# Convolution attention in query halves: two key tiles of the weighted sum together, three score banks, four single maxima banks

## The chip, the cores and the metric

The kernel runs on one core of one Trainium2 chip. The metric is the device time of one execution in microseconds. All the work of the change lies in one of the program's phases, the attention inside the convolution layer.

## What is computed

The whole program is a convolution layer with attention, then a second attention layer and a feed-forward layer. The change touches the first attention alone. For each of 8 images and 8 heads (head dimension 8, 1024 tokens), cut from the reference:

```python
logits = jnp.einsum('bnid,bnjd->bnij', qf, kf)      # 1024 x 1024 per head
logits = logits + rel_w + rel_h                     # relative positions, width and height
weights = jax.nn.softmax(logits, axis=-1)
attn = jnp.einsum('bnij,bnjd->bnid', weights, vf)
```

The softmax needs the maximum of each query's row before the exponentials can be taken.

## The kernel before, in words

`attention_phase` works in 16 groups (image by half of the heads), each of `HG` = 4 heads, `TT` = 8 tiles of 128 tokens and two query halves of `HALF` = 512 tokens. The relative positions are folded into the matmul: `qf` and `kf` hold 120 rows, and a 121st row of `qf` (`ROW_M`) carries minus the maximum of each query.

Each group is handled twice.

- **The first pass** finds the maxima, one group ahead of the rest. `logits` multiplies a query tile with all 1024 keys into one of two `sm` tensors, each two PSUM banks wide (two matmuls, L664). VectorE reduces its 1024 columns to `nmax` (`logits_max`, L644). That makes 32 steps a group. After the 16 steps of a pair of heads, the unit called "turn" transposes the pair's `nmax` on TensorE (L679), VectorE copies it to `mrow` (L657), and SyncE sends eight small DMAs that put it into row `ROW_M` of `qf` (`maxima`, L639).
- **The second pass** computes the scores transposed, keys on the partitions: `scores` (L880) writes one of two `st` banks, one per query half; ScalarE takes the exponential into `probs` (L855); `weighted` (L895) multiplies four heads' `probs` with the values `va` into `pv`. The four heads use 32 columns of the array each and run beside each other. These matmuls are fp32, and the trace shows each as two, so one call is 8 records: two waves of four.

Every engine runs its own queue in program order, and semaphores tie them. TensorE's order is written by hand in `period`, for each pair of (key tile, head) steps:

```python
for half in range(2):
    scores(n, j, s, half)
weighted(n, j, t - 1, h // 2)
for half in range(2):
    scores(n, j, s + 1, half)
for step in (s, s + 1):
    for half in range(2):
        first_pass(pe, n + 1, (j + 1) % BUFS, ahead, step, half)
```

So a group has 16 such rounds, each of four score matmuls, one weighted call and four first-pass matmuls. `scores` waits for the exponential of two matmuls before (`exp_done`), `logits` for the reduction two steps before (`sm_read`), and a turn for the last reduction of its pair. A turn comes twice a group, at first-pass steps 12 and 28 (16 and 32 less `AHEAD` = 4). The last group has no first pass beside it. The groups run in a loop of three (`all_groups`), four times around, with the first and the rest written out.

The first pass of group 0 runs earlier, in a block of its own, together with the matmuls of the relative positions; its order is the list `order`.

Of the kernel before, what the change touches and what calls it, by code (L numbers as in the profile page):

```python
# [11 lines left out]
P = 128  # L12
# [529 lines left out]
def attention_phase(nc, q_all, bd_hi, bd_lo, shared, first_stored, kq_d, rel_d, va_d, att_d):  # L542
# [12 lines left out]
    with ExitStack() as ctx:  # L555
# [7 lines left out]
        kf = [sb(f"a_kf{i}", [P, HG, TOK], f32r) for i in range(BUFS - 1)]  # L563
        nmax = sb("a_nmax", [P, HG, TT])
        mrow = sb("a_mrow", [2 * TT, HG // 2, P], f32r)

        sm = [ctx.enter_context(nc.psum_tensor(f"a_sm{i}", [P, TOK], f32)) for i in range(2)]
# [5 lines left out]
        sm_done, sm_read = sem("a_sm_done"), sem("a_sm_read")  # L573
# [9 lines left out]
        def first_pass_units(whole):  # L583
            units, step = [], 0
            for d, h, t in [(0, h, t) for h in range(HG) for t in range(TT)][AHEAD:] + [(1, 0, t) for t in range(AHEAD) if whole]:
                if t == 0 and h % 2 == 0:
                    units.append((step, "turn", 0, (h - 1) % HG, 0))
                units.append((step, "logits", d, h, t))
                step += 1
            return units if whole else units + [(step, "turn", 0, HG - 1, 0)]  # L590
        first_pass_of = {whole: first_pass_units(whole) for whole in (True, False)}
        NU = len(first_pass_of[True])
        unit_at = {whole: {unit[1:]: k for k, unit in enumerate(units)} for whole, units in first_pass_of.items()}
        units_before = lambda n: AHEAD + n * NU
        STEPS = TT * HG
        NS = 2 * STEPS

# [35 lines left out]
        def maxima(sp, n, j, whole):  # L633

            for h in range(HG):
                for half in range(2):
                    if half == 0:
                        sp.wait_ge(sm_read, units_before(n) + unit_at[whole]["turn", 0, h | 1, 0] + 1)
# [3 lines left out]
        def logits_max(dve, before, k, h, t):  # L642
            dve.wait_ge(sm_done, before + k + 1)
            nc.vector.tensor_reduce(nmax[:, h, t:t + 1], sm[k % 2][:], axis=AX.X, op=ALU.max, negate=True).then_inc(sm_read, 1)  # L644

        def first_pass_maxima(dve, n, whole, only=None):
            for k, (step, what, d, h, t) in enumerate(first_pass_of[whole]):
                if only not in (None, step):
                    continue
                if what == "logits":  # L650
                    logits_max(dve, units_before(n), k, h, t)
                else:
                    dve.wait_ge(sm_done, units_before(n) + k + 1)
# [3 lines left out]
                    nc.vector.tensor_copy(mrow[:, h // 2, :], sm[k % 2][0:2 * TT, 0:P]).then_inc(sm_read, 1)  # L657

        def logits(pe, j, before, k, h, t, half):

            if half == 0 and not (isinstance(before, int) and before + k < 2):
                pe.wait_ge(sm_read, before + k - 1)
            cols = slice(half * HALF, (half + 1) * HALF)
            m = nc.tensor.matmul(sm[k % 2][:, cols], qf[j][0:ROW_M, h, half, t * P:(t + 1) * P],  # L664
                                 kf[j][0:ROW_M, h, cols], start=True, stop=True)
            if half == 1:
                m.then_inc(sm_done, 1)

        def first_pass(pe, n, j, whole, s, half, va_after=0):

            for k, (step, what, d, h, t) in enumerate(first_pass_of[whole]):
                if step == s and what == "logits":
# [3 lines left out]
                elif step == s and half == 0:  # L676
                    pe.wait_ge(sm_read, units_before(n) + k - 1)
                    pe.wait_ge(sm_read, units_before(n) + unit_at[whole]["logits", 0, h, TT - 1] + 1)
                    nc.tensor.transpose(sm[k % 2][0:2 * TT, 0:P], nmax[:, h - 1:h + 1, :].rearrange("p h t -> p (h t)"), ident[:]).then_inc(sm_done, 1)  # L679
# [12 lines left out]
        passes = [("logits", 0, t) for t in range(AHEAD)] + [("pass", s, None) for s in range(STEPS)]  # L692
# [11 lines left out]
        with (nc.sbuf_tensor("a_hl", [P, 2, LAST, TOK], f32r) as own_hl, nc.psum_tensor("a_rel0", [P, 4, LAST, W], f32) as r0,  # L704
# [51 lines left out]
            def _(dve):  # L756
# [4 lines left out]
                for what, i, n in order:  # L761
# [5 lines left out]
                    elif what == "logits":  # L767
                        logits_max(dve, 0, n, 0, n)
                    else:
                        first_pass_maxima(dve, 0, True, i)  # L770

            @block.tensor
            def _(pe):
                for what, i, n in order:
# [15 lines left out]
                    for half in range(2):  # L790
                        if what == "logits":
                            logits(pe, 0, 0, n, 0, n, half)
                        else:
                            first_pass(pe, 0, 0, True, i, half, va_after=16)
# [4 lines left out]
        probs = bits(shared[:])  # L799
        out = sb("a_out", [P, TOK])  # L800
        st = [ctx.enter_context(nc.psum_tensor(f"a_st{i}", [P, HALF], f32)) for i in range(2)]
        pv = ctx.enter_context(nc.psum_tensor("a_pv", [P, TOK], f32))

        with nc.Block() as block:  # L804
# [36 lines left out]
            def _(act):  # L841
                def copy_out(n, half):
                    cols = slice(half * HALF, (half + 1) * HALF)
                    act.wait_ge(pv_done, n * 2 * TT + 2 * TT + 3 + half)
                    if half == 0:
                        act.wait_ge(out_stored, n * 16 + 16)
                    nc.scalar.activation(out[:, cols], pv[:, cols], ACT.Copy).then_inc(out_ready, 1)

                def period(n, j, more, ahead):
                    for u in range(NS):  # L850
                        t, h, half = u // (2 * HG), u // 2 % HG, u % 2
                        act.wait_ge(st_done, n * NS + u + 1)
                        if h == half == 0:
                            act.wait_ge(pv_done, n * 2 * TT + 2 * t + 2)
                        nc.scalar.activation(probs[:, t % 2, h, half * HALF:(half + 1) * HALF], st[half][:], ACT.Exp  # L855
                                             ).then_inc(exp_done, 1)
                        if u in (3, 7) and not (isinstance(n, int) and n == 0):
                            copy_out(n - 1, u // 4)

                all_groups(act, period)  # L860
                for half in range(2):
                    copy_out(NG - 1, half)
# [10 lines left out]
            def _(pe):  # L873
                def scores(n, j, s, half):

                    t, h = s // HG, s % HG
                    pe.wait_ge(exp_done, n * NS + 2 * s + half + 1)
                    if t == half == 0:
                        pe.wait_ge(max_loaded[h], n * 32 + 32)
                    nc.tensor.matmul(st[half][:], kf[j][0:ROW_M + 1, h, t * P:(t + 1) * P],  # L880
# [3 lines left out]
                def weighted(n, j, t, half):  # L884


                    if half == 0:
                        pe.wait_ge(exp_done, n * NS + 2 * HG * (t + 1) + 2)
                    if t == half == 0:
                        pe.wait_ge(loaded[j], times_loaded(n, j))  # L890
                    if t == 0:
                        pe.wait_ge(out_ready, n * 2 + half + 1)
                    cols = slice(half * HALF, (half + 1) * HALF)
                    for h in range(HG):
                        m = nc.tensor.matmul(pv[32 * h:32 * h + 32, cols], va[j][:, t, h, :], probs[:, t % 2, h, cols],  # L895
# [3 lines left out]
                def period(n, j, more, ahead):  # L899
                    for s in range(0, STEPS, 2):  # L900
                        t, h = s // HG, s % HG
                        for half in range(2):
                            scores(n, j, s, half)
                        if t:
                            weighted(n, j, t - 1, h // 2)
                        elif not (isinstance(n, int) and n == 0):
                            weighted(n - 1, (j - 1) % BUFS, TT - 1, h // 2)
                        for half in range(2):
                            scores(n, j, s + 1, half)
                        if more:  # L910
                            for step in (s, s + 1):
                                for half in range(2):
                                    first_pass(pe, n + 1, (j + 1) % BUFS, ahead, step, half)

                pe.sem_inc(exp_done, 2)
# [3 lines left out]
                for half in range(2):  # L919
                    weighted(NG - 1, (NG - 1) % BUFS, TT - 1, half)  # L920
# [952 lines left out]
```

## Time and profile before

| | us |
|---|---|
| runs | 2534.36, 2540.37, 2546.37 (median 2540.37) |
| span of the profiled execution | 2543.5 |
| part in which the groups run | 647 to 1475 |
| block before it, with the first pass of group 0 | 545 to 647 |

The profile gives no other time of its execution than its span, which lies 3.1 us above the median and inside the three runs. In the profile, DVE is VectorE, ACT ScalarE, PE a matmul and PEld its weight load; an entry like "[0.25 <-DVE a_nmax L644]" is the time that the engine stood idle just before, and what ended it. One row may merge several instructions (x4).

### The profile page before, as it was taken

Reading aid. Unit: us, or ns where it says so; the run is one execution under the profiler, and the core shown is the slowest. Engines: PE = TensorE matmul, PEld = TensorE weight load, DVE = VectorE, ACT = ScalarE, POOL = GpSimd, SP = SyncE. Lnnn points to the kernel's source line nnn. Section 1 sums busy time; section 2 is a strip of 40 time slices with the busy share of each in tenths; the row PEclk is TensorE's granted clock in tenths of the full one; section 3 lists DMA queues with packets and bytes.
Section 4 is the critical chain, followed back from the end, with each engine's and each line's share of the span. In section 5 each row is a group of like instructions: output and inputs, shape, how many; then the busy total and the mean of one; then the engine's idle time right before and its main releaser. Section 6 shows DMA issues by size and latency. Waiting matters only on the chain. (4 is left out here: it accounts for less than half of the span.)

```text
span 2543.5 us, 33099 instructions
## 1 busy us (share of the span) xinstructions
PE 2209.1 (87%) x10534; PEld 1523.3 (60%) x10534; DVE 1506.6 (59%) x2238; ACT 1188.2 (47%) x2087; POOL 332.1 (13%) x161
## 2 busy tenths in 40 slices
PE   4999999846899999999999838888888948888885
PEld 3778888745445454544554316777777736676664
DVE  6222433326677777777777214665556448888885
ACT  2111222212567676766777725555555434444342
POOL 1000000000000000000000012222222024444443
PEclk7999999855899999999999969999999979999988
DMA  2222243495757665676564033232221142222221
GB/s 78 87 62 80 85 157 132 133 162 198 153 91 123 106 105 92 112 117 99 101 107 73 9 86 111 96 97 94 95 95 50 50 130 83 84 83 83 83 89 52
DMA packets 155219, 249.54 MB, mean 98 GB/s; under 512 B 30912, under 2 KB 101312, under 8 KB 155072
## 3 DMA queue, kind: packets, MB, share of 16 engines
q1 hardware_dynamic: 153760, 247.05, 40.2%
q8 instruction: 75, 1.23, 0.2%
q10 hardware_dynamic: 1312, 0.67, 0.1%
q14 instruction: 72, 0.59, 0.1%
HBM read 154.52 MB, written 90.47 MB: 96 GB/s over the span
## 5 line engine op out<-in xcount | busy, mean ns | idle before, releaser
L644 DVE TENSOR_REDUCE a_nmax<-a_sm 128x1 f32<-128x1024 f32 x512 | 603.7, 1219 | 221.7 <-PE a_sm L664 221.5
L855 ACT ACTIVATE shared<-a_st 128x512 f32<-128x512 f32 x1024 | 556.6, 596 | 256.1 <-PE a_st L880 254.5
L895 PE MATMUL a_pv<-shared,a_va 128*32 128x512 f32 x2048 | 274.0, 608 | 0.9 <-ACT shared L855 0.9
L880 PE MATMUL a_st<-a_qf,a_kf 121*128 121x512 f32 x704 | 255.3, 440 | 18.8 <-issue 8.5
L664 PE MATMUL a_sm<-a_kf,a_qf 120*128 120x512 f32 x704 | 218.5, 429 | 57.5 <-DMA a_kf<-kq_d 32.9
L880 PEld LDWEIGHTS a_st<-a_qf,a_kf 121*128 121x128 f32 x704 | 120.1, 190 | 219.0 <-ACT shared L855 197.7
L664 PEld LDWEIGHTS a_sm<-a_kf,a_qf 120*128 120x128 f32 x704 | 136.0, 203 | 95.4 <-issue 33.0
L1707 ACT ACTIVATE x_hid<-x_h_ps,x_b 128x512 f32<-128x512 f32 x128 | 87.5, 689 | 213.5 <-DVE x_h_lo L1744 129.0
L1744 DVE SCALAR_TENSOR_TENSOR x_h_lo<-x_hid,x_wts,x_h_hi 128x512 fp32r<-128x512 f32 x128 | 175.3, 1370 | 9.6
L1742 DVE TENSOR_SCALAR x_h_hi<-x_hid,x_wts 128x512 fp32r<-128x512 f32 x128 | 114.9, 898 | 45.3 <-ACT x_hid L1707 40.4
L1153 POOL MEMSET b_wp<- 128x128 f32 x1 | 0.2, 204 | 977.5 <-POOLq L804 977.5
L1785 PE MATMUL x_h_ps<-x_v_hi,x_w_hi 128*128 128x512 f32 x256 | 106.7, 417 | 17.7 <-POOL x_w_lo L1673 17.4
L1355 PE MATMUL b_o_ps<-b_pT,b_v 128*128 128x256 f32 x512 | 120.7, 379 | 0.0
L1276 DVE TENSOR_REDUCE b_nmax<-b_s_ps 128x1 f32<-128x1024 f32 x64 | 78.4, 1224 | 69.4 <-PE b_s_ps L1340 62.8
L1799 PE MATMUL x_y_ps<-x_h_hi,x_w_hi 128*128 128x512 f32 x256 | 103.2, 403 | 17.9 <-DVE x_h_lo L1744 17.9
L507 PE MATMUL c_acc<-c_y_hi,c_w_hi 128*128 128x512 f32 x288 | 117.6, 408 | 0.0
L507 PE MATMUL c_acc<-c_y_hi,c_w_hl 128*128 128x512 f32 x288 | 117.2, 407 | 0.0
L507 PE MATMUL c_acc<-c_y_lo,c_w_hi 128*128 128x512 f32 x288 | 117.1, 407 | 0.0
L507 PE MATMUL c_acc<-c_y_lo,c_w_hl 128*128 128x512 f32 x288 | 117.1, 407 | 0.0
L507 PE MATMUL c_acc<-c_y_hi,c_w_lo 128*128 128x512 f32 x288 | 117.1, 406 | 0.0
L1186 ACT ACTIVATE b_probs<-b_s_ps,b_nmax 128x1024 f32<-128x1024 f32 x64 | 71.3, 1113 | 95.8 <-DVE b_nmax L1276 95.8
L880 PE MATMUL a_st<-q_all,a_kf 121*128 121x512 f32 x320 | 112.5, 433 | 0.3 <-ACT shared L855 0.3
(253 smaller groups left out, 4045.6 us busy)
## 6 DMA issues: line engine op xcount, KB each, us to landing
rel_d<-shared SPq DMA_DIRECT2D x12, 2048.0 KB, 12.2
a_qf<-rel_d SPq DMA_DIRECT2D x44, 512.0 KB
x_w_st<-in_L_ffn_W SPq DMA_DIRECT2D x32, 512.0 KB, 5.9
a_qf<-rel_d SPq DMA_DIRECT2D x44, 256.0 KB
q_all<-rel_d SPq DMA_DIRECT2D x20, 512.0 KB
a_qf<-kq_d SPq DMA_DIRECT2D x66, 128.0 KB
c_xtok<-in_x SPq DMA_DIRECT2D x8, 1024.0 KB, 5.6
va_d<-c_va SPq DMA_DIRECT2D x16, 512.0 KB, 4.8
```

What stands on the lines that cost most here:

```text
L507: m = nc.tensor.matmul(image_rows(acc[u][:]), wt[:, k, :] if tap is None else wt[:, k, tap, :], y[s][:, k, rows + dy:rows + dy + H // 2, d ...
L644: nc.vector.tensor_reduce(nmax[:, h, t:t + 1], sm[k % 2][:], axis=AX.X, op=ALU.max, negate=True).then_inc(sm_read, 1)
L664: m = nc.tensor.matmul(sm[k % 2][:, cols], qf[j][0:ROW_M, h, half, t * P:(t + 1) * P], kf[j][0:ROW_M, h, cols], start=True, stop=True)
L855: nc.scalar.activation(probs[:, t % 2, h, half * HALF:(half + 1) * HALF], st[half][:], ACT.Exp).then_inc(exp_done, 1)
L880: nc.tensor.matmul(st[half][:], kf[j][0:ROW_M + 1, h, t * P:(t + 1) * P], qf[j][0:ROW_M + 1, h, 2 * t // TT, half * HALF:(half + 1) * HALF ...
L895: m = nc.tensor.matmul(pv[32 * h:32 * h + 32, cols], va[j][:, t, h, :], probs[:, t % 2, h, cols], start=t == 0, stop=t == TT - 1, skip_gro ...
L1355: m = nc.tensor.matmul(o_ps[:], v_sb[s][:, t, :], pT[k % 2][:, t, :], start=t == 0, stop=t == TT - 1)
L1707: nc.scalar.activation(hid[k % 2][:], h_ps[k % 2][:], ACT.Gelu, bias=b1_sb[s][:, e, f:f + 1]).then_inc(hid_ready, 1)
L1742: nc.vector.tensor_scalar(h_hi[k % HB][:], hid[k % 2][:], wts[s][:, e:e + 1], None, ALU.mult)
L1744: nc.vector.scalar_tensor_tensor(h_lo[k % HB][:], hid[k % 2][:], wts[s][:, e:e + 1], bits(h_hi[k % HB][:]), ALU.mult, ALU.subtract).then_i ...
L1785: m = nc.tensor.matmul(h_ps[k % 2][:], w[s][:, e, c, tile(f)], v[s][:, c, half(j)], start=i == 0, stop=i == 3 * KC - 1)
L1799: m = nc.tensor.matmul(y_ps[j][c][:], w[s][:, e, f, tile(c)], h[k % HB][:], start=first and i == 0, stop=last and i == 2)
```

## The change

Nothing changes in what is computed. Parts:

- **First pass in halves.** `sm` is four tensors of one bank (`SB` = 4) in place of two of two banks. A step is now half the keys: one matmul, one reduction of 512 columns into `nmax_half`. There are 64 steps a group. After a pair's last reduction VectorE drains and takes the minimum of both halves (`tensor_tensor`, 128x16) into `nmax`, and signals `nmax_ready`, for which the turn waits. Turns stand at steps 24 and 56 and take two bank slots.
- **Second pass by query halves.** All 8 key tiles for the first 512 queries, then all 8 for the second. A unit is one matmul of one head; three `st` banks (`STB` = 3) are used in turn; `pv` is one bank; `probs` has four slots.
- **TensorE's order** is a string for each batch of 8 score units (8 batches a group): s is a score matmul, m a first-pass step, v a weighted call.
- ScalarE copies `pv` out after the 8th and the 40th exponential of a group, before after the 4th and the 8th.

```diff
+        SB = 4
+        sm = [ctx.enter_context(nc.psum_tensor(f"a_sm{i}", [P, HALF], f32)) for i in range(SB)]
...
+        STB = 3
+        SLOTS = 4
+        BATCH = 2 * HG
+        NB = NS // BATCH
+        ORDER = "mssmsmsvvsmsmmsmsm"
...
-            nc.vector.tensor_reduce(nmax[:, h, t:t + 1], sm[k % 2][:], axis=AX.X, op=ALU.max, negate=True).then_inc(sm_read, 1)
+            nc.vector.tensor_reduce(nmax_half[:, half, h, t:t + 1], sm[k % SB][:], axis=AX.X, op=ALU.max, negate=True).then_inc(sm_read, 1)
+            if h % 2 and t == TT - 1 and half:
+                dve.drain()
+                nc.vector.tensor_tensor(nmax[:, h - 1:h + 1], nmax_half[:, 0, h - 1:h + 1], nmax_half[:, 1, h - 1:h + 1], ALU.min
+                                        ).then_inc(nmax_ready, 1)
...
-            if half == 0 and not (isinstance(before, int) and before + k < 2):
-                pe.wait_ge(sm_read, before + k - 1)
+            if not (isinstance(before, int) and before + k < SB):
+                pe.wait_ge(sm_read, before + k + 1 - SB)
...
+                    pe.wait_ge(sm_read, units_before(n) + k + 1 - SB)
+                    pe.wait_ge(nmax_ready, n * (HG // 2) + (h + 1) // 2)
+                    nc.tensor.transpose(sm[k % SB][0:2 * TT, 0:P], nmax[:, h - 1:h + 1, :].rearrange("p h t -> p (h t)"), ident[:]).then_inc(sm_done, 2)
...
-        st = [ctx.enter_context(nc.psum_tensor(f"a_st{i}", [P, HALF], f32)) for i in range(2)]
-        pv = ctx.enter_context(nc.psum_tensor("a_pv", [P, TOK], f32))
+        st = [ctx.enter_context(nc.psum_tensor(f"a_st{i}", [P, HALF], f32)) for i in range(STB)]
+        pv = ctx.enter_context(nc.psum_tensor("a_pv", [P, HALF], f32))
...
+                def scores(n, j, u):
+
+                    half, t, h = u // (TT * HG), u // HG % TT, u % HG
+                    pe.wait_ge(exp_done, n * NS + u + 1)
...
+                    for i in range(NB):
+                        place = dict.fromkeys("smv", 0)
+                        for what in ORDER:
+                            k = place[what]
+                            place[what] += 1
+                            if what == "s":
+                                scores(n, j, i * BATCH + k)
+                            elif what == "m" and more:
+                                first_pass(pe, n + 1, (j + 1) % BUFS, ahead, i * BATCH + k)
+                            elif what == "v" and i:
+                                weighted(n, j, 2 * (i - 1) + k)
+                            elif what == "v" and not (isinstance(n, int) and n == 0):
+                                weighted(n - 1, (j - 1) % BUFS, 2 * (NB - 1) + k)
```

On TensorE, one round of before in the middle of a group reads as follows (a_st are the score banks, a_sm the first-pass ones, a_pv the weighted sum; a REGISTER_ALU works out what a wait compares with):

```order
L895 MATMUL a_pv<-shared,a_va0 32x512 x4
L877 REGISTER_ALU
L880 MATMUL a_st0<-a_qf0,a_kf0 128x512
L877 REGISTER_ALU
L880 MATMUL a_st1<-a_qf0,a_kf0 128x512
L662 REGISTER_ALU
L664 MATMUL a_sm1<-a_kf1,a_qf1 128x512 x2
L662 REGISTER_ALU
L664 MATMUL a_sm0<-a_kf1,a_qf1 128x512 x2
L877 REGISTER_ALU
L880 MATMUL a_st0<-a_qf0,a_kf0 128x512
L877 REGISTER_ALU
```

The same engine after the change, the middle of a batch:

```order
L896 MATMUL a_st1<-q_all,a_kf2 128x512
L678 REGISTER_ALU
L680 MATMUL a_sm0<-a_kf0,a_qf0 128x512
L893 REGISTER_ALU
L896 MATMUL a_st2<-q_all,a_kf2 128x512
L909 MATMUL a_pv<-shared,a_va2 32x512 x8
L893 REGISTER_ALU
L896 MATMUL a_st0<-q_all,a_kf2 128x512
L678 REGISTER_ALU
L680 MATMUL a_sm1<-a_kf0,a_qf0 128x512
```

Two weighted calls now stand together, once in 8 score matmuls rather than one in 4, and score and first-pass matmuls alternate.

At a turn, TensorE before (the rows ahead of the transpose are the weighted call and the two scores that follow it; the last first-pass matmul stands two scores ahead of that call):

```order
L880 MATMUL a_st0<-a_qf0,a_kf0 128x512
L877 REGISTER_ALU
L880 MATMUL a_st1<-a_qf0,a_kf0 128x512
L895 MATMUL a_pv<-shared,a_va0 32x512 x4
L877 REGISTER_ALU
L880 MATMUL a_st0<-a_qf0,a_kf0 128x512
L877 REGISTER_ALU
L880 MATMUL a_st1<-a_qf0,a_kf0 128x512
L677 REGISTER_ALU
L678 REGISTER_ALU
L679 MATMUL a_sm1<-a_ident,a_nmax 16x128
```

and after the change:

```order
L896 MATMUL a_st0<-q_all,a_kf2 128x512
L678 REGISTER_ALU
L680 MATMUL a_sm1<-a_kf0,a_qf0 128x512
L694 REGISTER_ALU
L695 REGISTER_ALU
L696 MATMUL a_sm2<-a_ident,a_nmax 16x128
L678 REGISTER_ALU
L680 MATMUL a_sm0<-a_kf1,a_qf1 128x512
```

The pair's last first-pass matmul (L680) now stands directly ahead of the transpose that waits for its reduction; four scores and a weighted call stood between them before.

## Rows read from the trace of the kernel before

**Rows 1.** The page: engines' busy time; two groups (busy, mean ns | idle before).

```profile
PE 2209.1 (87%) x10534; PEld 1523.3 (60%) x10534; DVE 1506.6 (59%) x2238; ACT 1188.2 (47%) x2087; POOL 332.1 (13%) x161
...
L644 DVE TENSOR_REDUCE a_nmax<-a_sm 128x1 f32<-128x1024 f32 x512 | 603.7, 1219 | 221.7 <-PE a_sm L664 221.5
L855 ACT ACTIVATE shared<-a_st 128x512 f32<-128x512 f32 x1024 | 556.6, 596 | 256.1 <-PE a_st L880 254.5
```

**Rows 2.** Windows: busy time in two steady groups and the last.

```profile
core 0: us, PE busy (x) PEld busy (x) DVE busy (x) ACT busy (x) POOL busy (x), PEclk, DMA share, GB/s
776.90:827.13 50.23, 50.15 (x258) 25.11 (x258) 38.24 (x35) 35.54 (x67) 0.00 (x0) 1.00 0.66 108
...
1425.20:1474.80 49.60, 41.61 (x196) 12.82 (x196) 0.00 (x0) 35.08 (x66) 0.00 (x0) 1.00 0.03 11
```

**Rows 3.** SyncE's timeline: start of the maxima DMAs of two following groups.

```profile
776.90 27.74 SPq L639 DMA_DIRECT2D a_qf<-a_mrow  x8
...
827.13 27.65 SPq L639 DMA_DIRECT2D a_qf<-a_mrow  x8
```

**Rows 4.** Timeline of one round (start us, us, engine ..., [idle before]).

```profile
936.47 1.06 PE L895 MATMUL a_pv<-shared,a_va 128*32 128x512 f32 x8
937.46 0.30 PEld L880 LDWEIGHTS a_st<-q_all,a_kf 121*128 121x128 f32 x2 [0.84 <-ACT shared L855]
938.00 1.09 ACT L855 ACTIVATE shared<-a_st 128x512 f32<-128x512 f32 x2 [0.53 <-PE a_st L880]
...
938.70 2.35 DVE L644 TENSOR_REDUCE a_nmax<-a_sm 128x1 f32<-128x1024 f32 x2 [0.75 <-PE a_sm L664]
...
939.14 0.19 PEld L880 LDWEIGHTS a_st<-q_all,a_kf 121*128 121x128 f32 x1 [0.22 <-ACT shared L855]
939.41 1.08 ACT L855 ACTIVATE shared<-a_st 128x512 f32<-128x512 f32 x2 [0.32 <-PE a_st L880]
...
939.58 1.07 PE L895 MATMUL a_pv<-shared,a_va 128*32 128x512 f32 x8
```

**Rows 5.** Timeline of the next round in short windows.

```profile
940.03 0.61 PE L895 MATMUL a_pv<-shared,a_va 128*32 128x512 f32 x4
940.57 0.19 PEld L880 LDWEIGHTS a_st<-q_all,a_kf 121*128 121x128 f32 x1 [0.84 <-ACT shared L855]
...
941.14 0.40 PE L664 MATMUL a_sm<-a_kf,a_qf 120*128 120x512 f32 x1
...
941.14 1.10 PE L664 MATMUL a_sm<-a_kf,a_qf 120*128 120x512 f32 x4
```

**Rows 6.** Timeline at a turn, and a small VectorE operation (ns min/median/max).

```profile
826.32 0.09 PEld L679 LDWEIGHTS a_sm<-a_ident,a_nmax 128*16 128x16 f32 x1 [0.24 <-DVE a_nmax L644]
826.82 0.28 DVE L657 CAST a_mrow<-a_sm 16x128 fp32r<-16x128 f32 x1 [0.56 <-PE a_sm L679]
827.15 0.30 PEld L664 LDWEIGHTS a_sm<-a_kf,a_qf 120*128 120x128 f32 x2 [0.50 <-DVE a_mrow L657]
...
L50 DVE TENSOR_TENSOR b_tmp<-b_tmp,b_var x16: 161/164/166, 1515.9 to 1964.9; 128x4 f32<-128x4 f32 x16
```

**Rows 7.** Timeline of a round in the last group.

```profile
1430.32 0.30 PEld L880 LDWEIGHTS a_st<-a_qf,a_kf 121*128 121x128 f32 x2 [0.84 <-ACT shared L855]
...
1431.51 0.19 PEld L880 LDWEIGHTS a_st<-a_qf,a_kf 121*128 121x128 f32 x1 [0.89 <-ACT shared L855]
...
1433.41 0.30 PEld L880 LDWEIGHTS a_st<-a_qf,a_kf 121*128 121x128 f32 x2 [0.84 <-ACT shared L855]
```

**Rows 8.** Timeline and windows after three gaps on TensorE (columns of Rows 2).

```profile
858.82 0.31 PEld L880 LDWEIGHTS a_st<-a_qf,a_kf 121*128 121x128 f32 x2 [3.05 <-issue]
...
860.50:863.40 2.90, 2.90 (x10) 2.17 (x7) 0.59 (x1) 1.60 (x4) 0.00 (x0) 0.50 0.00 0
...
2131.16 0.50 PE L1799 MATMUL x_y_ps<-x_h_hi,x_w_hi 128*128 128x512 f32 x1 [1.97 <-DVE x_h_lo L1744]
2131.00:2133.00 2.00, 1.66 (x6) 1.05 (x6) 1.93 (x5) 1.27 (x2) 0.00 (x0) 1.00 0.72 248
...
2303.21 0.50 PE L1799 MATMUL x_y_ps<-x_h_hi,x_w_hi 128*128 128x512 f32 x1 [2.17 <-DVE x_h_lo L1744]
2304.20:2307.20 3.00, 2.70 (x10) 1.89 (x10) 2.92 (x6) 0.91 (x2) 0.00 (x0) 0.50 0.56 131
```

More of the change, by code:

```diff
@@ L586, in first_pass_units @@
                 if t == 0 and h % 2 == 0:
[L587 to L590, printed above, removed]
-        first_pass_of = {whole: first_pass_units(whole) for whole in (True, False)}
[L592 to L596, printed above, removed]
+                    units.append((step, "turn", 0, (h - 1) % HG, 0, 0))
+                units.append((step, "logits", d, h, t, 0))
+                units.append((step + 1, "logits", d, h, t, 1))
+                step += 2
+            return units if whole else units + [(step, "turn", 0, HG - 1, 0, 0)]
+        first_pass_of = {whole: first_pass_units(whole) for whole in (True, False)}
+        slots = {"logits": 1, "turn": 2}
+        slot_of = {whole: [sum(slots[u[1]] for u in units[:k]) for k in range(len(units))] for whole, units in first_pass_of.items()}
+        NU = sum(slots[u[1]] for u in first_pass_of[True])
+        slot_at = {whole: {unit[1:]: slot_of[whole][k] for k, unit in enumerate(units)} for whole, units in first_pass_of.items()}
+        units_before = lambda n: 2 * AHEAD + n * NU
+        STEPS = 2 * TT * HG
+        NS = STEPS
+        STB = 3
[3 more added lines that the diff above has]
+        ORDER = "mssmsmsvvsmsmmsmsm"
         def all_groups(eng, period):
@@ L656, in first_pass_maxima, with first_pass @@
                             dve.wait_ge(max_loaded[head], n * 32)
-                    nc.vector.tensor_copy(mrow[:, h // 2, :], sm[k % 2][0:2 * TT, 0:P]).then_inc(sm_read, 1)
+                    nc.vector.tensor_copy(mrow[:, h // 2, :], sm[k % SB][0:2 * TT, 0:P]).then_inc(sm_read, 2)
         def logits(pe, j, before, k, h, t, half):
-            if half == 0 and not (isinstance(before, int) and before + k < 2):
-                pe.wait_ge(sm_read, before + k - 1)
+            if not (isinstance(before, int) and before + k < SB):
+                pe.wait_ge(sm_read, before + k + 1 - SB)
             cols = slice(half * HALF, (half + 1) * HALF)
[L664 to L672, printed above, removed]
+            nc.tensor.matmul(sm[k % SB][:], qf[j][0:ROW_M, h, half, t * P:(t + 1) * P],
+                             kf[j][0:ROW_M, h, cols], start=True, stop=True).then_inc(sm_done, 1)
+        def first_pass(pe, n, j, whole, s, va_after=0):
+            for u, (step, what, d, h, t, half) in enumerate(first_pass_of[whole]):
+                if step != s:
+                    continue
+                k = slot_of[whole][u]
+                if what == "logits":
                     if d == 1 and t == half == 0:
@@ L675, in first_pass @@
                     logits(pe, (j + d) % BUFS, units_before(n), k, h, t, half)
[L676 to L679, printed above, removed]
+                else:
+                    pe.wait_ge(sm_read, units_before(n) + k + 1 - SB)
+                    pe.wait_ge(nmax_ready, n * (HG // 2) + (h + 1) // 2)
+                    nc.tensor.transpose(sm[k % SB][0:2 * TT, 0:P], nmax[:, h - 1:h + 1, :].rearrange("p h t -> p (h t)"), ident[:]).then_inc(sm_done, 2)
         def times_loaded(n, j):
@@ L691, in attention_phase @@
         rels = [("rel", r, n) for r in range(len(RELS)) for n in range(RU)]
-        passes = [("logits", 0, t) for t in range(AHEAD)] + [("pass", s, None) for s in range(STEPS)]
+        passes = [("logits", 0, t) for t in range(AHEAD)] + [("pass", s, None) for s in range(STEPS // 2)]
         order = rels[:LOAD_UNITS]
@@ L766, in _ @@
                                                 rel_target(bits(hl[i % 2][:, 0]), wh, n), ALU.subtract).then_inc(rel_lo, 1)
[L767 to L770, printed above, removed]
+                    for half in range(2):
+                        if what == "logits":
+                            logits_max(dve, 0, 2 * n + half, 0, n, half)
+                        elif what == "pass":
+                            first_pass_maxima(dve, 0, True, 2 * i + half)
             @block.tensor
@@ L842, in copy_out @@
                 def copy_out(n, half):
-                    cols = slice(half * HALF, (half + 1) * HALF)
-                    act.wait_ge(pv_done, n * 2 * TT + 2 * TT + 3 + half)
+                    act.wait_ge(pv_done, n * 2 * TT + TT * (half + 1) + 4)
                     if half == 0:
                         act.wait_ge(out_stored, n * 16 + 16)
-                    nc.scalar.activation(out[:, cols], pv[:, cols], ACT.Copy).then_inc(out_ready, 1)
+                    nc.scalar.activation(out[:, half * HALF:(half + 1) * HALF], pv[:], ACT.Copy).then_inc(out_ready, 1)
                 def period(n, j, more, ahead):
                     for u in range(NS):
-                        t, h, half = u // (2 * HG), u // 2 % HG, u % 2
                         act.wait_ge(st_done, n * NS + u + 1)
[L853 to L858, printed above, removed]
+                        if u % BATCH == 0:
+                            act.wait_ge(pv_done, n * 2 * TT + 2 * (u // BATCH) + 2)
+                        nc.scalar.activation(probs[:, u // HG % SLOTS, u % HG], st[(j + u) % STB][:], ACT.Exp).then_inc(exp_done, 1)
+                        if u == BATCH - 1 and not (isinstance(n, int) and n == 0):
+                            copy_out(n - 1, 1)
+                        if u == NS // 2 + BATCH - 1:
+                            copy_out(n, 0)
                 all_groups(act, period)
-                for half in range(2):
-                    copy_out(NG - 1, half)
+                copy_out(NG - 1, 1)
             @block.vector
@@ L899, in period @@
                 def period(n, j, more, ahead):
[L900 to L915, printed above, removed]
+                    for i in range(NB):
[11 more added lines that the diff above has]
+                                weighted(n - 1, (j - 1) % BUFS, 2 * (NB - 1) + k)
+                pe.sem_inc(exp_done, STB)
                 pe.sem_inc(pv_done, 4)
@@ L918, in _ @@
                 all_groups(pe, period)
-                for half in range(2):
-                    weighted(NG - 1, (NG - 1) % BUFS, TT - 1, half)
+                for k in range(2):
+                    weighted(NG - 1, (NG - 1) % BUFS, 2 * (NB - 1) + k)
 def self_attention_phase(nc, x, attn_w, attn_b, w_q, w_k, w_v, w_o, b_o, mixT_d, att_d, rsum_d, t_d, vT_d, vsum_d):
```

41 lines of the change are left out of this document (19 added, 22 removed).

## The prediction

> **What bounds the kernel now.** I read the page first: TensorE is busy 87% of the span [rows 1], and the part in which the groups run is 828 us of it. The windows come next: in a steady group TensorE is busy 50.15 of 50.23 us, VectorE 38.24, ScalarE 35.54 [rows 2]. The maxima DMAs of two following groups start 827.13 - 776.90 = 50.23 us apart, so that is a group's time [rows 3]. A busy TensorE says nothing about which limit it runs at, so I read one round of the timeline.
>
> A round lasts 939.58 - 936.47 = 3.11 us; I use 3.10. In it, per TensorE [rows 4, 5]:
>
> - Four first-pass matmuls take 1.10 us where one alone takes 0.40, so each further one costs (1.10 - 0.40) / 3 = 0.234 us. Eight such matmuls (four first-pass, four scores) are 1.87.
> - A weighted call's second wave starts at 940.03, 0.45 after the first (939.58), and the next weight load starts at 940.57. From the call's start to that load is 0.99 us, and the load itself (0.19) lies bare ahead of its matmul. A call thus costs 1.18 to 1.19.
> - 1.87 + 1.19 = 3.06. The remaining 0.04 to 0.05 is the wait for ScalarE: the load at 939.14 stood 0.22 us idle, of which some 0.17 would have been hidden under the matmul before.
>
> So TensorE's own work is nearly all of the round. A second chain is equally long, though: in the last group, where no first pass stands between, the round is still 1433.41 - 1430.32 = 3.09 us [rows 7]. There it is the two score banks: load, exponential (0.54 us later), the next load into the same bank after it. Both limits end together. VectorE has slack: two reductions of 1024 columns take 2.35 us (the second starts some 1.14 after the first, though one lasts 1.219) out of 3.10 [rows 1, 4].
>
> **The change, on TensorE.** A batch of 8 scores and 8 first-pass matmuls replaces two rounds, 6.20 us. The matmuls stay 16 x 0.234 = 3.74. The two weighted calls stand together, so the bare load and the changeover are paid once: 1.19 + 2 x 0.45 = 2.09. No row shows two calls in a row; below, the array's streaming can't be cut, and I put 0.85 for the second at least (0.427 a wave would be the 512 columns at two passes, which the 0.45 row nearly is); above, nothing is saved and it costs 1.19. I take 0.90, since it repeats the measured wave. Batch: 5.83 us, group 8 x 5.83 = 46.6 against 16 x 3.10 = 49.6.
>
> The third score bank must carry ScalarE over the 2.1 us of the calls. Two exponentials take 1.08 where one takes 0.596, so each further one costs 0.49 [rows 1, 4]; eight are 3.9 of 5.83. Walking through a batch with each score waiting for the exponential three before, no wait is over 0.02 us, except behind a copy of `pv` (0.5 more on ScalarE), where the score three later waits about 0.3. Two copies a group: 0.6. At 0.545 per exponential in place of 0.49 it would be 0.6 more.
>
> **The change, on VectorE.** No row has a 512-column reduction. The 1024-column one lasts 1.219 us, and the copy of 128 columns 0.28 [rows 1, 6]; the difference, 0.94 us for 896 columns, is 1.05 ns a column. So 512 columns last 1.219 - 0.534 = 0.685 us, and if the next one again starts 0.08 before the end, each costs 0.605. Eight are 4.84 of 5.83: VectorE is not the bound in a plain batch. The bounds are 0.57 (half the spacing of 1.14) and 0.685 (no overlap).
>
> Now the turns. In the new order a turn's transpose directly follows the last first-pass matmul of its pair, and needs its reduction, and then the drain and the minimum. Let 0 be the time of the first weight load after the calls. The matmuls s m s m m s m s m then begin at 0.19, 0.42, 0.66, 0.89, 1.13, 1.36, 1.59, 1.83, 2.06. A result reaches VectorE 0.35 after its beginning (a load at 937.46 has its exponential at 938.00, 0.54 later, of which the load is 0.19 [rows 4]). The five reductions begin at 0.77, 1.38, 1.98, 2.59 and 3.19, because each comes sooner than the one before is done; the last ends at 3.88. Add 0.05 for the drain, 0.164 for the minimum [rows 6] and 0.05 for the semaphore: the transpose can load at 4.15. Without a turn the next load would be at 2.11, so TensorE stands still for about 2.05 us, and the transpose costs 0.1 to 0.2 more. A turn costs 2.2 us. Queued behind it on TensorE are all the scores, so ScalarE idles too; VectorE idles until the next first-pass matmul, and what it catches up is of no use, since it had slack. The least that it could be, if VectorE had no backlog at the last matmul, is 0.35 + 0.685 + 0.26 = 1.3. Before, the transpose waited 0.24 [rows 6], and a group's two turns cost 50.23 - 49.6 = 0.63 together: four scores and a weighted call stood in between as cover, and the change takes this cover away.
>
> **Sum.** A group: 46.6 + 2 x 2.2 + 0.6 = 51.6, against 50.23: +1.4. That holds for the 15 groups with a first pass beside them: +21. The last group has none; there three banks help: walking it through with the same numbers, a batch of 8 scores and two calls takes 5.48 us against 6.20, so 8 x 0.72 = 5.8 less, and the two copies give back 1.0: -4.8. At the very end one copy of `pv` remains where there were two: -0.5. In the block before the groups the same matmuls and columns run beside the position matmuls at the low clock; 13 steps there are bound by VectorE, 2 x 0.605 against 1.22 to 1.27 each, which with the drains is 0. The loop's four turnarounds stay (below). Total: +16.
>
> The clock may add to it. At the loop's turnaround a gap of 3.05 us is followed by a stretch at a granted clock of 0.50, that is 1.2 GHz, of 3 us; TensorE had full clock before it [rows 8]. Of two gaps close to the new one, that of 1.97 us left it at 1.00 (2.4 GHz), and that of 2.17 us was followed by 0.50 for 3 us [rows 8]. A slow stretch costs up to half its length, 1.5 us. There are 30 turns beside the scores; I put one in ten of them slow: 30 x 0.1 x 1.5 = +5. The sum is +21 on the profiled span of 2543.5; on the median, 2540.4 + 21 = 2561 us.
>
> The Trainium skill has a rule against this change (VectorE: DVE Perf Modes, section The DRAIN you can't avoid): each VectorE instruction empties its pipe before the next begins, so one should have fewer instructions. The trace disagrees in size, since its second reduction starts before the first one's recorded end. By that rule the 512-column reduction would cost its full 0.685 each, and the time would be that of the second case below.
>
> **The rivals.**
>
> - VectorE becomes the bound. With 0.685 for each reduction, 64 of them are 43.8 us a group, and two turns with their drains, transposes and copies, in which it waits, some 2.5 each; the same walk gives 54 us a group. 15 x 3.9 - 5 = +53: 2594 us. For it: twice as many instructions, each with its own wait. Against: the overlap of 0.08 that the pairs show now. It decides from 0.65 us on.
> - Every turn's gap lowers the clock: 16 + 30 x 1.5 = +61: 2600 us. For it: the gap of 2.17 us. Against: that of 1.97 us.
> - The stall is short. If VectorE is not behind at the last matmul, a turn costs 1.5: 50.2 a group, and only the last group counts: 2540 - 5 = 2535 us, no change. Against: five results come within 1.64 us, and each takes at least 0.57.
> - Faster: the alternation of score and first-pass matmuls lets TensorE step faster than 0.234 us. The weight load of 0.19, which runs under the matmul before, and the 512 columns at 2.4 GHz (0.213) leave room down to 0.213. Then a batch is 16 x 0.213 + 2.09 = 5.50, a group 8 x 5.50 + 4.4 + 0.6 = 49.0, and 15 x -1.2 - 5 = -23: 2517 us. It decides from 0.225 on. Against: the same 0.234 holds in the four first-pass matmuls, half of which have no wait of their own.
>
> **How the numbers follow.** The median of runs here spreads by 0.24% to both sides, so 0.5%, 13 us, is about what can be told from no change. Chances: forecast 0.50 (range 2548 to 2575; a fifth of it is within 13 us), VectorE the bound 0.12, clock 0.08, short stall 0.15, faster 0.15. Slower by over 0.5%: 0.40 + 0.12 + 0.08 = 0.60. Within: 0.10 + 0.13 = 0.23. Faster: 0.15 + 0.02 = 0.17. For the range I leave out the upper end of the clock case and the lower half of the faster one: 2520 to 2600.
>
> **What would show it.** In the profile after: the 512-column reduction lasts 0.685 us and pairs start 0.605 apart; the two weighted calls take 1.9 us from start to the next load; a plain batch 5.8 to 5.9 us; the transpose's load has an idle time of about 2 us put down to VectorE's minimum, twice a group; groups 51 to 52.5 us apart. It is wrong if the transpose waits less than 1 us, if a plain batch is off 5.83 by more than 0.2, or if the score loads wait for ScalarE in every batch.

## The result

The changed kernel takes 2769.55 us (median; 2762.3 to 2776.12), before 2540.93: a ratio of 1.0897 (95% interval 1.0871 to 1.0922). It is 229 us slower, where 21 were forecast, and lies far outside the stated range.

The page of the changed kernel, its engines and the groups that answer to [rows 1]:

```profile
PE 2246.6 (81%) x10534; PEld 1568.5 (57%) x10534; DVE 1544.2 (56%) x2782; ACT 1179.6 (43%) x2087; POOL 332.6 (12%) x161
...
L655 DVE TENSOR_REDUCE a_nmax_half<-a_sm 128x1 f32<-128x512 f32 x1024 | 634.3, 683 | 413.9 <-PE a_sm L680 412.6
L871 ACT ACTIVATE shared<-a_st 128x512 f32<-128x512 f32 x1024 | 546.9, 602 | 349.3 <-PE a_st L896 336.9
```

No engine has much more work: TensorE and VectorE are busy some 38 us longer each. All are idle more, so the time is in waits. The 512-column reduction lasts 0.683 us, as worked out (0.685). Next the windows, over one group (the maxima DMAs of two following groups start at 998.28 and 1066.17):

```profile
core 0: us, PE busy (x) PEld busy (x) DVE busy (x) ACT busy (x) POOL busy (x), PEclk, DMA share, GB/s
998.30:1066.20 67.90, 51.45 (x260) 27.63 (x260) 40.39 (x69) 35.01 (x66) 0.00 (x0) 0.88 0.50 80
```

A group takes 67.9 us against 50.23 [rows 2], and TensorE stands idle for 16.4 of them; the mean clock is 0.88. But a plain batch is as forecast. Its weight loads on TensorE, from one batch's first load after the calls to the next one's (1008.67 - 1002.78 = 5.89 us, forecast 5.83), with the two calls between 1006.82 and 1008.67 (1.85 us, forecast 1.90):

```profile
1002.78 0.19 PEld L896 LDWEIGHTS a_st<-q_all,a_kf 121*128 121x128 f32 x1 [0.84 <-issue]
...
1006.82 0.16 PEld L909 LDWEIGHTS a_pv<-shared,a_va 128*32 128x32 f32 x8 [0.24 <-issue]
...
1008.67 0.19 PEld L896 LDWEIGHTS a_st<-q_all,a_kf 121*128 121x128 f32 x1 [0.84 <-ACT shared L871]
```

So is the turn: the minimum ends at 997.33, the transpose loads at 997.45, and TensorE's loads had been idle 2.31 us:

```profile
997.16 0.17 DVE L658 TENSOR_TENSOR a_nmax<-a_nmax_half 128x16 f32<-128x16 f32 x1
997.45 0.09 PEld L696 LDWEIGHTS a_sm<-a_ident,a_nmax 128*16 128x16 f32 x1 [2.31 <-issue]
997.48 0.27 PE L696 MATMUL a_sm<-a_ident,a_nmax 128*16 128x128 f32 x1 [1.90 <-DVE a_nmax L658]
```

The rest shows in the waits, from 650 to 1690 us (total, times, longest), in a wait that the prediction has no word of:

```profile
ACT a_out L864 <- DMA att_d<-a_out: 148.7, 13, 14.6
```

The copy of `pv` waits for the store of the group before. Behind each of these 13 waits the clock is low as well, 0.50 to 0.67 in the 5 us after it, as here:

```profile
1093.60:1098.60 5.00, 4.53 (x18) 1.12 (x19) 0.00 (x0) 1.90 (x4) 0.00 (x0) 0.50 0.00 0
```

In the timeline of one group, SyncE issues that store at 992.25, after all 18 loads of the group after next; it lands 31.7 us later, and until then ScalarE, and behind it TensorE, stand still:

```profile
990.74 1.15 SPq L642 DMA_DIRECT2D a_kf<-kq_d  x3
992.25 0.39 SPq L847 DMA_DIRECT2D att_d<-a_out  x1
...
1024.00 0.60 ACT L864 ACTIVATE a_out<-a_pv 128x512 f32<-128x512 f32 x1 [12.54 <-DMA att_d<-a_out]
...
1025.14 0.80 PE L896 MATMUL a_st<-q_all,a_kf 121*128 121x512 f32 x1 [12.63 <-ACT shared L871]
```

The kernel before had the same slow store; only nothing needed it soon. Its full DMA list (KB each, median us to landing) says so. The page of the profile shows only the largest issues and leaves this row out, and the prediction doesn't use it:

```profile
att_d<-a_out SPq DMA_DIRECT2D x16, 512.0 KB, 30.9
```

There, both copies of group n's `pv` follow the end of group n, so the store of group n-1 had a whole group, some 37 us after its issue (issued at 771.45, next copy at 808.72), in which to land. Now the first half's copy of group n comes after 40 of 64 exponentials of group n itself: in the group shown it is due 19 us after the issue (1024.00 - 12.54 - 992.25).

### The profile page after: what moved, and what is told of

Same layout as the page of the kernel before. It is cut to its first block and busy times, and to the rows that moved or that the text cites. A ratio compares the mean times of both kernels' runs of the same rounds, so it can differ in the third digit from the quotient of the medians.

```text
span 2774.4 us, 34499 instructions
## 1 busy us (share of the span) xinstructions
PE 2246.6 (81%) x10534; PEld 1568.5 (57%) x10534; DVE 1544.2 (56%) x2782; ACT 1179.6 (43%) x2087; POOL 332.6 (12%) x161
## 5 line engine op out<-in xcount | busy, mean ns | idle before, releaser
L655 DVE TENSOR_REDUCE a_nmax_half<-a_sm 128x1 f32<-128x512 f32 x1024 | 634.3, 683 | 413.9 <-PE a_sm L680 412.6
L871 ACT ACTIVATE shared<-a_st 128x512 f32<-128x512 f32 x1024 | 546.9, 602 | 349.3 <-PE a_st L896 336.9
L896 PE MATMUL a_st<-a_qf,a_kf 121*128 121x512 f32 x704 | 298.4, 447 | 106.9 <-ACT shared L871 106.7
L680 PE MATMUL a_sm<-a_kf,a_qf 120*128 120x512 f32 x704 | 283.7, 448 | 55.6 <-DMA a_kf<-kq_d 33.2
L909 PE MATMUL a_pv<-shared,a_va 128*32 128x512 f32 x2048 | 285.6, 681 | 0.0
L896 PEld LDWEIGHTS a_st<-a_qf,a_kf 121*128 121x128 f32 x704 | 140.8, 201 | 234.3 <-ACT shared L871 180.2
L680 PEld LDWEIGHTS a_sm<-a_kf,a_qf 120*128 120x128 f32 x704 | 145.6, 211 | 106.5 <-DVE a_nmax_half L655 49.8
L896 PE MATMUL a_st<-q_all,a_kf 121*128 121x512 f32 x320 | 134.8, 443 | 46.7 <-ACT shared L871 46.6
L909 PEld LDWEIGHTS a_pv<-shared,a_va 128*32 128x32 f32 x2048 | 58.4, 121 | 142.3 <-issue 86.2
L680 PE MATMUL a_sm<-a_kf,q_all 120*128 120x512 f32 x320 | 122.4, 416 | 12.0 <-issue 8.4
L896 PEld LDWEIGHTS a_st<-q_all,a_kf 121*128 121x128 f32 x320 | 63.9, 200 | 99.6 <-ACT shared L871 74.1
```

The source lines that it names most:

```text
L655: nc.vector.tensor_reduce(nmax_half[:, half, h, t:t + 1], sm[k % SB][:], axis=AX.X, op=ALU.max, negate=True).then_inc(sm_read, 1)
L680: nc.tensor.matmul(sm[k % SB][:], qf[j][0:ROW_M, h, half, t * P:(t + 1) * P], kf[j][0:ROW_M, h, cols], start=True, stop=True).then_inc(sm_ ...
L871: nc.scalar.activation(probs[:, u // HG % SLOTS, u % HG], st[(j + u) % STB][:], ACT.Exp).then_inc(exp_done, 1)
L896: nc.tensor.matmul(st[(j + u) % STB][:], kf[j][0:ROW_M + 1, h, t * P:(t + 1) * P], qf[j][0:ROW_M + 1, h, 2 * t // TT, half * HALF:(half + ...
L909: m = nc.tensor.matmul(pv[32 * h:32 * h + 32, :], va[j][:, t, h, :], probs[:, w % SLOTS, h], start=t == 0, stop=t == TT - 1, skip_group_ch ...
```

## The experiments

**Theory A**: the early copy waits for a store behind the loads; that is the loss beyond the sum. Rivals: **B**, the loss is VectorE's or the turns' and the store wait only takes time that would be lost anyway; **C**, the store is slow whatever its place.

**1. Store in halves.** Each half of `out` has its own store and semaphore; the first half's is issued between the two pairs of maxima DMAs.

```diff
-                        store(n - 1)
+                        store(n - 1, 1)
                     if more:
-                        maxima(sp, n + 1, (j + 1) % BUFS, ahead)
+                        maxima(sp, n + 1, (j + 1) % BUFS, ahead, range(2))
+                    store(n, 0)
+                    if more:
+                        maxima(sp, n + 1, (j + 1) % BUFS, ahead, range(2, HG))
...
-                    if half == 0:
-                        act.wait_ge(out_stored, n * 16 + 16)
+                    act.wait_ge(out_stored[half], n * 16 + 16)
```

> The changed kernel with out stored in two halves, each with its own semaphore: the store of the first half is issued between the two pairs of maxima DMAs, so a copy of pv waits for a store issued nearly a whole group before. Theory A (the early copy of pv waits for a store that stands behind the loads in the DMA queues, 148.7 us in 13 waits, and the low clock after each): that wait is gone, and the sum of the prediction stands, 2561 us (2550 to 2580), groups 51 to 52.5 us apart. Rival B (the loss is VectorE's or the turns', and the store wait only takes time that would be lost anyway): over 2650 us.

Measured: 2591.45 us (2590.36 to 2593.45), ratio to before 1.020 (1.018 to 1.0221). The wait is gone from the list, and 178 of the 229 us with it: A holds and B falls. Of the 178, 148.7 are the wait itself; the other 29 fit the low clock behind each wait, but were not parted from it. And 2591 is 11 us above the expected range and 30 above the sum: the groups are 53 to 55 us apart, not 51 to 52.5.

**2. Store first.** One line moved on SyncE.

```diff
+                    if not (isinstance(n, int) and n == 0):
+                        store(n - 1)
                     if ahead:
                         load(n + 2, (j + 2) % BUFS)
-                    if not (isinstance(n, int) and n == 0):
-                        store(n - 1)
```

> The changed kernel with one line moved on SyncE: the store of a group ahead of the loads of the group after next. Theory A: the store is slow only because it stands behind 4.6 MB of loads; issued first it lands in 3 to 6 us and the copy does not wait; 2561 to 2585 us, the loads starting 3 us later. Rival C (the store itself is slow, or the transfers compete whatever their order): landing stays near 30 us and the time near 2770 us.

Measured: 2613.74 us (2605.53 to 2616.71), ratio 1.0289 (1.0268 to 1.0311). The DMAs' time to landing (min/median/max) is now a tenth, so the store is not slow by itself and C falls:

```profile
DMA to landing us min/median/max: 2.6/2.8/3.1
```

It is 22 us slower than the half stores and 29 above the expected range. The loads start later, and in 7 places TensorE now waits for them, which is half of the 22 us; the rest was not traced:

```profile
PE a_sm L680 <- DMA a_kf<-kq_d: 10.9, 7, 3.8
```

**3. The wait alone, in the kernel before.**

```diff
                             copy_out(n - 1, u // 4)
+                        if u == NS // 2 + 7:
+                            act.wait_ge(out_stored, n * 16 + 16)
```

> The kernel before with only one wait added: after the 40th exponential of a group ScalarE waits until the store of the group before has landed. Nothing else is changed. Theory A: the store is issued 12.6 us into a group and lands 31 us later, at 43.7, while the 40th exponential is at 31; so 12 to 13 us are lost in each of 13 groups, and some more by the low clock after each gap: 2540 + 165 to 200 = 2705 to 2740 us. Rival B: the wait costs little by itself, under 2580 us.

Measured: 2756.55 us (2748.4 to 2758.31), ratio 1.0837 (1.0809 to 1.0864). One wait, with nothing else of the change, costs 213 us, nearly as much as the changed kernel loses. The size was expected 17 to 52 us too small; the waits are 15.5 us each, not 12 to 13:

```profile
ACT shared L855 <- DMA att_d<-a_out: 201.1, 13, 16.9
```

**4. One turn moved.** On top of the half stores: the unit "turn" of the first pair stands three first-pass steps later, after the weighted calls.

```diff
-                if t == 0 and h % 2 == 0:
-                    units.append((step, "turn", 0, (h - 1) % HG, 0, 0))
-                units.append((step, "logits", d, h, t, 0))
-                units.append((step + 1, "logits", d, h, t, 1))
-                step += 2
+                for half in range(2):
+                    due = 0 if d else 3
+                    if h % 2 == 0 and 2 * t + half == due:
+                        units.append((step, "turn", 0, (h - 1) % HG, 0, 0))
+                    units.append((step, "logits", d, h, t, half))
+                    step += 1
```

> The half stores, and the first of a group's two turns moved three first-pass steps later, behind the weighted calls; the second turn stays. If a turn costs 2.2 us because its reduction directly precedes it, the moved one costs 0.3 or less: 15 x 1.9 = 28 us less than the half stores alone, about 2533 us. If the gap at the turn is made of time that ScalarE or VectorE would need anyway, there is no change against the half stores alone.

Measured: 2553.2 us (2550.28 to 2561.77), ratio 1.0045 (1.0024 to 1.0066). That is 38 us less than with the half stores alone, where 28 were expected: 2.55 us a turn. The unmoved turn's transpose load still stands idle for 2.31 us (first row), the moved one's not at all:

```profile
905.76 0.09 PEld L697 LDWEIGHTS a_sm<-a_ident,a_nmax 128*16 128x16 f32 x1 [2.31 <-issue]
...
935.79 0.09 PEld L697 LDWEIGHTS a_sm<-a_ident,a_nmax 128*16 128x16 f32 x1
```

So a turn costs more than its stall. I read the granted clock in the 5 us after each of the 30 turns between 650 and 1500 us. With the half stores it is 0.66 to 0.68 in 22 of them and 1.00 in 8, and in the 2 us ahead of each of the 30 it is 1.00. Before, it is below 1 in one of 30, and that one holds another gap, a wait of 4.55 us for a DMA. Three windows with the half stores; the second shows the low stretch alone:

```profile
1023.60:1028.60 5.00, 4.96 (x24) 2.39 (x24) 2.35 (x4) 2.28 (x4) 0.00 (x0) 0.66 0.03 7
1024.60:1027.60 3.00, 3.00 (x13) 1.40 (x16) 1.85 (x3) 2.28 (x4) 0.00 (x0) 0.50 0.03 7
970.00:975.00 5.00, 4.99 (x29) 2.68 (x30) 2.58 (x5) 2.62 (x6) 0.00 (x0) 1.00 0.02 3
```

The next turn follows some 27.5 us after one with the low clock (828.8 to 856.4), 26.1 after one without (802.7 to 828.8). 22 x 1.4 = 31 us, which matches the 30 that were left over.

**5. The gap filled.** To part the clock from the stall: the half stores, and in each turn five matmuls without use, in the stall.

```diff
+                    for _ in range(5):
+                        nc.tensor.matmul(sm[k % SB][:], qf[j][0:ROW_M, h, 1, 0:P], kf[j][0:ROW_M, h, 0:HALF], start=True, stop=True)
                     pe.wait_ge(nmax_ready, n * (HG // 2) + (h + 1) // 2)
```

> The half stores, and in each turn five more matmuls of 512 columns into the turn's own bank, ahead of its wait for the minimum; their results are overwritten by the transpose. They use up 1.2 us of the 2 us stall and do no useful work. If 31 us of the half stores' time come from the low clock after 22 of 30 turns, this kernel is about 2560 us although it does more work. If the clock has nothing to do with it, it is 2591 us or more.

Measured: 2555.67 us (2553.73 to 2561.2), ratio 1.0056 (1.0036 to 1.0075). More work, 36 us less time than with the half stores. A turn's gap is 0.74 us now, and the clock in the 5 us after it is full in 29 of 30; the one low stretch, at 683.5, begins only after a further gap of 2.19 us, a wait for a DMA. The next turn follows after about 26.1 us (as 977.17 to 1003.26), just as after the full-clock turns without the filling, so within the groups the filling changes the clock and nothing else:

```profile
1003.26 0.27 PE L698 MATMUL a_sm<-a_ident,a_nmax 128*16 128x128 f32 x1 [0.74 <-DVE a_nmax L658]
...
1003.30:1008.30 5.00, 4.96 (x28) 2.50 (x29) 2.44 (x5) 2.48 (x5) 0.00 (x0) 1.00 0.06 18
```

But not all 36 us come from these 30 turns. Group 0's first pass, in the block before the groups, has two turns with the same filling. There the granted clock is 0.50 with the half stores and 1.00 with the filling, for 10 us at least (first row half stores, second filled), and the groups start 10 us sooner (636.3 against 646.6):

```profile
605.00:615.00 10.00, 8.65 (x35) 7.81 (x35) 7.75 (x13) 2.67 (x4) 0.00 (x0) 0.50 0.66 263
605.00:615.00 10.00, 9.75 (x67) 8.37 (x66) 9.47 (x17) 3.59 (x6) 0.00 (x0) 1.00 0.85 337
```

The part with the groups is 30 us shorter (877.9 against 847.5 us), which matches the 31 us of the clock. The rest of the program took 4 us longer in this execution. So the 2556 us here equal the forecast's sum without its clock term (2540.4 + 16) by luck.

**6. Both turns moved.** As in 4, with `due` = 3 for both.

> The half stores, with both turns three first-pass steps later, behind the weighted calls. A moved turn saved 38.25 / 15 = 2.55 us before (stall and low clock), so 38 us less than with one moved: 2515 us. Against it: the second turn's DMAs then have only some 2 us left before the next group's scores of heads 2 and 3 need them; if they are late by 0.5 to 1.5 us a group, 2523 to 2537 us.

Measured: 2565.66 us (2563.29 to 2575.92), ratio 1.0088 (1.0066 to 1.011): 12 us more than with one moved, a miss. The maxima DMAs are late as feared, 11.8 us in 20 waits, but the greater part is another wait, for the next group's keys (waits from 650 to 1480 us). It took 13.3 us in experiment 4 and takes 32.9 here:

```profile
PE a_sm L681 <- DMA a_kf<-kq_d: 32.9, 13, 3.9
PE a_st L902 <- DMA a_qf<-a_mrow: 7.8, 11, 1.5
...
PE a_st L902 <- DMA q_all<-a_mrow: 4.0, 9, 0.7
```

With the stalls gone the group is short, while the first-pass steps that read the next group keep their early place. In one group the loads' last issue is at 923.5 and that matmul runs at 955.92 after 3.42 us of waiting, 32.4 later. The transfers set the pace there. These gaps bring the low clock back: in the 5 us behind 10 of the last 12 waits for keys the granted clock is 0.50 to 0.69. The very last of the 30 turns is not moved by this edit.

**7. The order begun elsewhere.** On the half stores. The order is the same ring, cut at another place, so that a batch begins with a score and the calls, and a turn follows them; the copies of `pv` move up.

```diff
-        ORDER = "mssmsmsvvsmsmmsmsm"
+        ORDER = "svvsmsmmsmsmmssmsm"
...
-                        if u == BATCH - 1 and not (isinstance(n, int) and n == 0):
+                        if u == HG - 1 and not (isinstance(n, int) and n == 0):
...
-                        if u == NS // 2 + BATCH - 1:
+                        if u == NS // 2 + HG - 1:
```

> The half stores, with the same cyclic order of TensorE begun at another place (s v v s m ...), so that a turn always follows two scores and two weighted calls, and the copies of pv after the 4th and 36th exponential. Nothing is added. Theory: the turn's stall of 2 us and the low clock after it are gone, a group takes 47.3 us, 15 x (47.3 - 50.2) - 6 = -50: 2490 to 2505 us, faster than both. Rival: the second weighted call of a batch now comes 1.7 us after the batch's last score, and waits for its exponential; at 0.5 us in each batch that is 60 us, and the time is near 2550 us.

Measured: 2500.25 us (2489.83 to 2504.81), ratio 0.9824 (0.9797 to 0.9851), faster than both kernels. The transpose loads 0.20 us after the score's load, without a wait, and the group shown takes 47.63 us at full clock with TensorE busy throughout:

```profile
963.62 0.50 PE L901 MATMUL a_st<-a_qf,a_kf 121*128 121x512 f32 x1
963.96 0.27 PE L696 MATMUL a_sm<-a_ident,a_nmax 128*16 128x128 f32 x1
...
940.86:988.49 47.63, 47.59 (x260) 26.10 (x258) 39.73 (x69) 34.86 (x67) 0.00 (x0) 1.00 0.69 115
```

The 91 us less than with the half stores are in part idle time and in part clock. Over the part with the groups (half stores first), TensorE's idle time falls from 71.5 to 18.6 us, and its busy time by 41 us, at a mean granted clock of 0.94 and 0.98:

```profile
646.00:1524.50 878.50, 806.99 (x4054) 430.39 (x4054) 601.17 (x1012) 559.57 (x1057) 0.00 (x0) 0.94 0.54 92
646.00:1430.30 784.30, 765.70 (x4054) 410.15 (x4052) 592.62 (x1012) 557.86 (x1057) 0.00 (x0) 0.98 0.60 103
```

The next group's keys are needed 33 us after their issue here (907.49 to 940.22), with no wait in this group. The rival's wait did not come: the weight loads of the calls stand idle 111.6 us in all, against 128.1 with the half stores.

**8. The same order with the single store.** Experiment 7's edit on the changed kernel, without the half stores.

> The changed kernel with TensorE's order begun at the other place and the copies of pv after the 4th and 36th exponential, but with its single store, behind the loads. The order alone takes 91 us off the kernel with half stores (2591 to 2500). Theory: while the store sets the time, a group lasts until the store has landed (some 44 us into the group), and then the part after the copy, 28 of 64 units or 21 us, and 1.5 us of low clock: 66 to 67 us against 68.9 now. So most of the 91 us are not seen: 2730 to 2745 us. Rival: the gains add up, 2770 - 91 = 2680 us.

Measured: 2719.59 us (2710.14 to 2730.86), ratio 1.0702 (1.0655 to 1.075). Of the 91 us that this order brings with half stores, 50 are seen. ScalarE's wait for the store grows from 11.4 to 14.9 us each, in part because the copies themselves stand four exponentials earlier:

```profile
ACT a_out L864 <- DMA att_d<-a_out: 194.3, 13, 17.5
```

It falls between the theory's 2730 to 2745 and the rival's 2680, 10 us outside the theory's range. One account fits: the store's landing swallows what comes ahead of it in the group and lets through what comes behind. The first of the two turns stands ahead of the copy, the second behind, which fits a half; that was not tried apart, and remains an argument.

## Why the prediction was wrong

**The step that failed** is the walk through ScalarE's queue: "no wait is over 0.02 us, except behind a copy of `pv` (0.5 more on ScalarE)". It priced the copy by its duration and left out what the copy itself waits for, the store of the group before. The change moves the copy from after the group to its middle, and with it the point at which that store must have landed. This costs 178 us here (experiment 1) and 213 us alone (experiment 3): 13.7 and 16.4 us for each of 13 waits, low clock included. The trace of before had the row with the 30.9 us. The text ahead of the prediction even names the moved copies, but their sum has the copy's duration and no wait. None of the listed signs of being wrong looks at this wait either.

**The clock** was a right mechanism with a wrong size. "I put one in ten of them slow" gave 5 us; it was 22 of 30 at 1.4 us each, 31 us, and experiment 5 takes them away. Of the two gaps shown, those of 1.97 and 2.17 us, one was followed by the low clock and one not. The turn's gap of 1.90 us, always the same, has both outcomes too. Two rows, one of them low, gave no ground for one in ten.

**What held.** The plain batch: 5.83 forecast, 5.89 measured. The reduction: 0.685 and 0.683 us. The turn: 2.2 us forecast; the matmul after the transpose begins at 997.59 and would have at about 995.41, 2.2 later. Within it, the 0.05 us for the drain and 0.05 for the semaphore stood on no row; the gaps on both sides of the minimum are 0.09 and 0.12. The last group: 5.48 forecast, and one round of loads after the calls comes 1701.28 - 1695.85 = 5.43 after the last; but the two batches with a copy of `pv` take 7.4 (as 1659.02 to 1666.44), where 0.5 more was forecast, since the clock is low in them too. The sum: 16 us without its clock term. With the store wait gone, 2591.45 - 2543.85 - 31 = 17 are left (2543.85 is before, measured beside it); two full-clock turns make a group of 52.2 us, 51.6 forecast. The direction was right mostly by luck: the terms that the forecast names make up a fifth of the loss.

**The rivals.** VectorE is no bound: eight reductions take 4.87 us of 5.89 (0.60 apart, 0.683 each). The prediction gave half of what the Trainium skill says (VectorE: DVE Perf Modes, section The DRAIN you can't avoid): the same section adds that a next instruction "that is not held starts earlier". The overlap of 0.08 us in this trace agrees with that, so the skill gave no reason for the full 0.685 each. "Every turn's gap lowers the clock" was near for its own term (22 of 30), with a chance of 0.08. The short stall and the faster stepping did not come: matmuls in a batch still begin 0.23 apart.

| kernel | us | what the step says |
|---|---|---|
| before | 2541 | |
| changed | 2770 | |
| store wait gone (1) | 2591 | 178 us: store, with the low clock behind its waits |
| and gap filled (5) | 2556 | 36 us: clock, some 30 among the groups, the rest in the block before |
| or order begun elsewhere (7) | 2500 | 91 us: the turns' stall and clock; the moved copies not parted |

## What to carry to other kernels

When a change moves an instruction to an earlier place, read every wait in front of it and look up when that event happens, DMA landings above all: a buffer's release that was free a group later can be the bound. Here a transfer issued behind a queue of loads landed with them, so its time to landing, not its size, was its price. Where a producer's last result is needed by the next instruction of a full engine, see whether the same work cut at another point of its cycle puts other work between.

## What the runs showed of the hardware that was not expected

Gaps of 1.9 us on TensorE, each behind a stretch at a granted clock of 1.00, were followed by a stretch at 0.50 (1.2 GHz) in 22 of 30 cases, gaps of 0.74 us in the same place in none. The length of the gap alone does not decide it: in the last group of the changed kernel, where TensorE also waits several times in each batch, a gap of 0.47 us is followed by 0.50:

```profile
1662.66 0.50 PE L896 MATMUL a_st<-a_qf,a_kf 121*128 121x512 f32 x1 [0.47 <-ACT shared L871]
1664.50:1666.50 2.00, 2.00 (x13) 0.28 (x5) 0.00 (x0) 0.00 (x0) 0.00 (x0) 0.50 0.00 0
```

Matmuls whose result is thrown away gained 36 us net: among the groups by closing the gaps, and in the block before by a clock of 1.00 where it had been 0.50. A 512 KB store landed in 2.8 us ahead of the loads and in 29 to 31 us (medians) behind them.
